# Log-sparse attention block with a spiking feed-forward: ScalarE measures four groups of entering rows and makes all marks, the base product is split in two halves, and every engine's order is rewritten

## The reference

```python
def attn(x):                       # 16 heads of 8
    q, k, v = x @ Wq.T + bq, x @ Wk.T + bk, x @ Wv.T + bv
    scores = where(mask, q . k, 0.0) / sqrt(8)   # mask: key j = i, or i - 2**m, m = 0..9
    return softmax(scores) @ v @ Wo.T + bo       # masked keys keep weight exp(0)
def ffn(x):
    y = square(relu(x @ W_fc.T)) @ W_proj.T      # 128 -> 512 -> 128
    # five leaky steps with threshold 1 and reset; the mean number of spikes
    return count_of_spikes(y) / 5
x = x + layernorm(attn(layernorm(x)))
x = x + layernorm(ffn(layernorm(x)))
```

## Time and profile before

| what | value |
|---|---|
| median of 3 runs | 229.02 us |
| the profiled execution's own time | 228.11 us |
| its span in the trace | 226.3 us |
| mean granted clock of TensorE | 0.91 of full |
| PE busy | 184.1 us (81%) |
| DVE busy | 180.6 us (80%) |
| POOL busy | 161.8 us (72%) |
| ACT busy | 111.6 us (49%) |
| DMA | 30.51 MB, mean 135 GB/s |

### The profile page before, as it was taken

The page is one execution under the profiler, slowest core; times in us unless marked ns, Lnnn a source line. Parts: engine busy times, 40 slices in busy tenths (PEclk is TensorE's granted clock), DMA queues, the critical chain, the costliest instruction groups (busy, mean ns, idle before and its releaser), DMA issues.

```text
span 226.3 us, 3606 instructions
## 1 busy us (share of the span) xinstructions
PE 184.1 (81%) x1108; PEld 93.4 (41%) x1108; DVE 180.6 (80%) x451; ACT 111.6 (49%) x311; POOL 161.8 (72%) x197
## 2 busy tenths in 40 slices
PE   7688985739090998778999999499997799999961
PEld 2223523212020643532645634364464366364840
DVE  5869999999999959999569986760598679866562
ACT  2354755410010035595589468315982725655980
POOL 7342228776799959999999999489297997835031
PEclk9969999985769569999999999758999999999997
DMA  6920000599897899983944399798586710100002
GB/s 183 263 66 0 0 3 1 146 212 216 197 217 197 209 233 225 232 183 107 219 104 127 86 224 234 218 227 209 130 198 142 158 33 0 49 1 23 26 24 69
DMA packets 18388, 30.51 MB, mean 135 GB/s; under 512 B 2753, under 2 KB 15042, under 8 KB 16322
## 3 DMA queue, kind: packets, MB, share of 16 engines
q10 hardware_dynamic: 4176, 22.22, 43.3%
q1 hardware_dynamic: 14194, 8.07, 13.3%
HBM read 25.17 MB, written 5.11 MB: 134 GB/s over the span
## 4 chain that ended last, share of the span: by engine, by line
PE 30%; POOL 28%; DVE 16%; DMA 10%; issue 9%; ACT 3%; ACTq 1%; SPq 1%; POOLq 1%; DVEq 0%
POOL ws L662 15%; DMA packed<-wt 8%; DVE qk L869 5%; PE xbank L1187 5%; PE xbank L1178 5%; PE xbank L1168 4%; POOL wt L601 3%; PE xbank L1163 3%; POOL wt L612 3%; DVE qk L875 3%; DVE ws L930 2%; DMA x_all<-x 2%; PE q_bank L1178 2%; PE q_bank L1187 2%; PE v_bank L1178 2%
## 5 line engine op out<-in xcount | busy, mean ns | idle before, releaser
L662 POOL TENSOR_TENSOR ws<-ws 128x1024 f32<-128x1024 f32 (+1 forms) x36 | 76.2, 2117 | 8.0 <-DVE ws L930 7.4
L930 DVE TENSOR_TENSOR ws<-v_bank,ws 128x896 f32<-128x896 f32 (+4 forms) x54 | 48.0, 905 | 3.8 <-DMA ws<-packed 3.8
L1137 PE MATMUL scores<-qk,head_sum 128*32 128x512 f32 (+1 forms) x256 | 28.0, 573 | 6.6 <-DVE es_raw L897 6.3
L1187 PE MATMUL xbank<-hid,wproj 128*128 128x512 f32 (+1 forms) x56 | 26.8, 577 | 1.2 <-ACT hid L799 1.2
L869 DVE SCALAR_TENSOR_TENSOR qk<-q_bank,bias_cols,kT 128x512 f32<-128x512 f32 (+9 forms) x40 | 24.8, 688 | 2.0 <-ACT kT L722 1.9
L1178 PE MATMUL xbank<-xnT_ff,wfc 128*128 128x512 f32 (+1 forms) x48 | 24.3, 598 | 1.8 <-ACT xnT_ff L713 1.2
L875 DVE SCALAR_TENSOR_TENSOR qk<-q_bank,bias_cols,kT 128x1024 f32<-128x1024 f32 x20 | 24.3, 1266 | 0.3 <-issue 0.2
L1168 PE MATMUL xbank<-wo,ws 128*64 128x128 f32 x264 | 23.9, 319 | 0.0
L1163 PE MATMUL xbank<-wo_base,ws_base 17*128 17x128 f32 x52 | 14.9, 373 | 9.9 <-POOL ws L662 6.7
L799 ACT ACTIVATE hid<-hid 128x512 f32<-128x512 f32 (+1 forms) x36 | 20.7, 581 | 1.6 <-POOL ws L662 1.1
L793 ACT ACTIVATE hid<-xbank 128x512 f32<-128x512 f32 (+1 forms) x24 | 13.4, 559 | 12.6 <-PE xbank L1178 8.0
(11 more groups left out here) (146 smaller groups left out, 345.9 us busy)
## 6 DMA issues: line engine op xcount, KB each, us to landing
ws<-packed ACTq DMA_DIRECT2D x16, 1024.0 KB, 7.6
ws<-packed ACTq DMA_DIRECT2D x4, 768.0 KB, 10.7
packed<-wt SPq DMA_DIRECT2D x16, 128.0 KB
ws<-packed ACTq DMA_DIRECT2D x4, 512.0 KB, 5.8
x_all<-x SPq DMA_DIRECT2D x7, 256.0 KB, 5.3
out<-x_all SPq DMA_DIRECT2D x7, 256.0 KB, 2.3
packed<-wt SPq DMA_DIRECT2D x4, 96.0 KB
x_all<-x SPq DMA_DIRECT2D x2, 128.0 KB, 3.3
```

Of the source, the lines that this page charges most:

```text
L662: e.tensor_tensor(out=a, in0=a, in1=b, op=ALU.add).then_inc(merged, 1)
L930: return v.tensor_tensor(out=w, in0=steps_of(tokens, o - o2, slots, [CH, i1 - i0], [1, CH]), in1=w, op=ALU.mult)
L1137: last = t.matmul(scores[32 * j:32 * j + 32, k, :], head_sum[:, half, :], qk[:, u % 2, k, tok:tok + CH], start=half == 0, stop=half == 1)
L1187: last = t.matmul(bank[:, 0:n], wproj[:, f, :], hid[:, g % 2, f, 0:n], start=f == 0, stop=f == FB - 1)
```

## The change

- `ON_DVE["in"] = (0, 1, 2, 7, 8)`: for entering groups 3, 4, 5, 6 DVE no longer measures the rows. ACT does, in the new stage `powers_in`: four Identity activations that accumulate the row sums, one that turns the sums into negative means, four Square activations with that mean as bias that accumulate the variance. POOL's `rsqrt in` then reads `power`, and for these groups makes no negative mean.
- `ON_DVE["marks"] = ()`: the marks of groups 4, 5, 6 are made by ACT (Sign) and no longer by DVE.
- `ON_POOL["square"] = (8,)`: the four squares of group 8 move from ACT to POOL. `FOLD = (7,)`: in group 7 POOL adds one more slot to another, and the attention there has one slot less.
- The base product of each block is issued as two products of 64 tokens, each 64 columns wide in its stationary operand.
- The warm-up is 28 matmuls of 256 columns on a tile of its own (before: 14 of 512). The `neg_ident` constant and the unused stage `shift` of PE are gone. `KEEP` is empty, so the new stage `keep_up` never runs.
- All five orders are rewritten, with other PSUM banks. Near the start, SP loads `wo` before the second group of `x` and the ffn weights after it; DVE makes both products, max and shift of unit 0 with only the measures of groups 7 and 8 between them, and starts weights 0 in the middle of unit 2's products; POOL's sum of unit 0 stands ahead of its differences, behind five `rsqrt in` where seven stood; ACT has `powers in` 3 and 4 around norm in 2, and 5 and 6 around the first spreads.

```diff
 ON_DVE = {
-    "marks": (4, 5, 6),
+    "in": (0, 1, 2, 7, 8),
+    "marks": (),
...
-ON_POOL = {"square": (), "sum": (0, 1, 2, 3)}
-FOLD = ()
-WARM = 14
+ON_POOL = {"square": (8,), "sum": (0, 1, 2, 3)}
+FOLD = (7,)
+WARM, KEEPS = 28, 8
...
 DVE_ORDER = (
...
+    ("centred bo", 0), ("centred fc", 0), ("moments in", 2), ("products 0", 0), ("products 1", 0),
+    ("moments in", 7), ("max", 0), ("moments in", 8), ("shift", 0), ("products 0", 1),
+    ("inverse", 0), ("products 1", 1), ("max", 1), ("shift", 1), ("products 0", 2), ("inverse", 1),
+    ("weights 0", 0), ("products 1", 2), ("weights 1", 0), ("max", 2), ("weights 2", 0),
...
             def rsqrt_in(g):
                 rsqrt("in", g)
+                if g not in ON_DVE["in"]:
+                    return
...
+            def powers_in(g):
+                u, first, n = IN_GROUPS[g]
+                done = upto(ON_DVE["in"], g, False)
+                act.wait_ge(x_in[g], 16)
...
+                for i in range(n):
+                    last = s.activation(squares["in"][:, i, :], rows(IN_GROUPS[g])[:, i, :], ACT.Identity,
+                                        accum_out=row_sums[:, g, i:i + 1])
...
+                s.activation(neg_mean[:, u, first:first + n], row_sums[:, g, 0:n], ACT.Identity,
+                             scale=-1.0 / (D * float(np.sqrt(D)))).then_inc(mean_by_act, 1)
...
+                for i in range(n):
+                    last = s.activation(squares["in"][:, i, :], rows(IN_GROUPS[g])[:, i, :], ACT.Square,
+                                        scale=1.0 / float(np.sqrt(D)), bias=neg_mean[:, u, first + i:first + i + 1],
+                                        accum_out=power["in"][:, g, i:i + 1])
...
-                    t.matmul(bank[:, cols], ws_base[:, h, (first + i) * P:(first + i + 1) * P],
-                             wo_base[:, u // 2 % 2, :], start=True, stop=False)
+                    for half in range(2):
+                        tok = (first + i) * P + CH * half
+                        t.matmul(bank[CH * half:CH * half + CH, cols], ws_base[:, h, tok:tok + CH],
+                                 wo_base[:, u // 2 % 2, :], start=True, stop=False)
```

The new orders around the end and the middle, as far as the prediction speaks of them:

```diff
 ACT_ORDER = (
...
+    ("square 0", 5), ("square 1", 5), ("signs", 4), ("relu 2", 5), ("norm ff", 6),
+    ("relu 3", 5), ("square 2", 5), ("square 3", 5), ("turned ff", 6), ("signs", 5), ("norm ff", 7),
...
+    ("square 3", 7), ("signs", 6), ("relu 0", 8), ("relu 1", 8), ("relu 2", 8), ("relu 3", 8),
+    ("signs", 7), ("signs", 8),
 POOL_ORDER = (
...
+    ("normalise 2", 5), ("rsqrt mid", 3), ("merge 1", 4), ("normalise 0", 6), ("merge 2", 4),
+    ("normalise 1", 6), ("merge 3", 4), ("normalise 2", 6), ("rsqrt ff", 3), ("rsqrt out", 1),
...
 PE_ORDER = (
...
+    ("up 2", 8, 4), ("down 2", 7), ("up 3", 8, 5), ("count", 6, 3), ("down 3", 7), ("down", 8, 0),
+    ("down 1", 8), ("down 2", 8), ("down 3", 8), ("count", 7, 1), ("count", 8, 4),
```

More of the change, by code:

```diff
@@ L88 @@
[L88 to L91, removed]
+    ("rsqrt in", 0), ("rsqrt in", 1), ("rsqrt in", 2), ("rsqrt in", 3), ("rsqrt in", 4), ("sum", 0),
+    ("differences", 0), ("normalise 0", 0), ("normalise 1", 0), ("normalise 2", 0), ("rsqrt in", 5),
@@ L92 @@
+    ("rsqrt ff", 7), ("rsqrt mid", 8), ("rsqrt out", 5), ("rsqrt ff", 8), ("square 0", 8),
+    ("square 1", 8), ("square 2", 8), ("square 3", 8), ("rsqrt out", 6), ("rsqrt out", 7),
+    ("rsqrt out", 8),
 )
 ACT_ORDER = (
-    ("norm in", 0), ("norm in", 1), ("turned in", 0), ("turned in", 1), ("keys", 0), ("norm in", 2),
-    ("turned in", 2), ("norm in", 3), ("keys", 1), ("turned in", 3), ("norm in", 4), ("norm in", 5),
-    ("total", 0), ("keys", 2), ("turned in", 4), ("base", 0), ("turned in", 5), ("keys", 3),
@@ L97 @@
[L97 to L114, removed]
@@ L115 @@
-    ("powers out", 2), ("signs", 3), ("spread 1", 7), ("norm ff", 4), ("turned ff", 4),
[8 rows of a table removed]
-    ("square 1", 8), ("signs", 7), ("relu 2", 8), ("square 2", 8), ("relu 3", 8), ("square 3", 8),
-    ("signs", 8),
+    ("norm in", 0), ("turned in", 0), ("norm in", 1), ("turned in", 1), ("keys", 0),
+    ("powers in", 3), ("norm in", 2), ("powers in", 4), ("turned in", 2), ("norm in", 3),
+    ("keys", 1), ("norm in", 4), ("exp", 0), ("turned in", 3), ("total", 0), ("turned in", 4),
+    ("keys", 2), ("base", 0), ("powers in", 5), ("total", 2), ("keys", 3), ("spread 0", 0),
@@ new lines @@
+    ("base", 2), ("norm in", 5), ("exp", 1), ("spread 1", 0), ("turned in", 5), ("spread 2", 0),
+    ("powers in", 6), ("keys", 4), ("norm in", 6), ("turned in", 6), ("spread 0", 1), ("exp", 2),
+    ("total", 4), ("spread 1", 1), ("keys", 5), ("spread 2", 1), ("norm in", 7), ("exp", 3),
+    ("spread 0", 2), ("powers mid", 0), ("spread 1", 2), ("spread 2", 2), ("powers ff", 0),
+    ("turned in", 7), ("keys", 6), ("exp", 4), ("spread 0", 3), ("norm ff", 0), ("spread 1", 3),
+    ("powers mid", 1), ("turned ff", 0), ("base", 4), ("norm in", 8), ("relu 0", 0),
@@ new lines @@
+    ("spread 2", 3), ("relu 1", 0), ("square 0", 0), ("relu 2", 0), ("square 1", 0),
+    ("turned in", 8), ("square 2", 0), ("powers ff", 1), ("relu 3", 0), ("keys", 7),
+    ("spread 0", 4), ("exp", 5), ("norm ff", 1), ("square 3", 0), ("spread 1", 4),
+    ("powers mid", 2), ("turned ff", 1), ("signs", 0), ("relu 0", 1), ("spread 2", 4),
+    ("relu 1", 1), ("square 0", 1), ("powers out", 0), ("square 1", 1), ("norm ff", 2),
+    ("relu 2", 1), ("exp", 6), ("square 2", 1), ("relu 3", 1), ("square 3", 1), ("spread 0", 5),
@@ new lines @@
+    ("powers mid", 3), ("spread 1", 5), ("turned ff", 2), ("relu 0", 2), ("square 0", 2),
+    ("signs", 1), ("relu 1", 2), ("square 1", 2), ("powers out", 1), ("spread 0", 6),
+    ("spread 2", 5), ("norm ff", 3), ("relu 2", 2), ("spread 1", 6), ("square 2", 2), ("relu 3", 2),
+    ("turned ff", 3), ("square 3", 2), ("powers mid", 4), ("relu 0", 3), ("exp", 7), ("relu 1", 3),
+    ("square 0", 3), ("relu 2", 3), ("square 1", 3), ("signs", 2), ("total", 6), ("relu 3", 3),
+    ("square 2", 3), ("base", 6), ("square 3", 3), ("spread 2", 6), ("norm ff", 4), ("spread 0", 7),
@@ L133 @@
[L133 to L138, removed]
@@ L157 @@
+    ("residual", 8), ("moments ff", 8), ("final", 5), ("moments out", 6), ("final", 6),
+    ("moments out", 7), ("moments out", 8), ("final", 7), ("final", 8),
 )
 PE_ORDER = (
-    ("warm", 0, 0), ("centre qkv", 0, 2), ("centre fc", 0, 1), ("turn in", 0, 0), ("turn in", 1, 2),
-    ("queries", 0), ("keys", 0, 0), ("values", 0), ("turn in", 2, 1), ("values", 1), ("keys", 1, 2),
-    ("turn in", 3, 0), ("scores 0", 0), ("queries", 1), ("scores 1", 0), ("keys", 2, 1),
-    ("total", 0, 2), ("turn in", 4, 0), ("base", 0), ("turn in", 5, 1), ("keys", 3, 0),
@@ L179 @@
[L179 to L180 removed]
[7 rows of a table removed]
[L188 removed]
+    ("warm", 0, 0), ("centre qkv", 0, 2), ("turn in", 0, 1), ("centre fc", 0, 0), ("turn in", 1, 2),
+    ("keys", 0, 1), ("values", 0), ("queries", 0), ("turn in", 2, 0), ("scores 0", 0),
+    ("scores 1", 0), ("keys", 1, 2), ("values", 1), ("turn in", 3, 1), ("queries", 1),
@@ L1202, in count, with keep_up @@
                 last.then_inc(count_filled, 1)
+            def keep_up(i):
+                what, u, j = KEEP[i]
+                bank = bank_for("keep", i)
+                if what == "products":
+                    pe.wait_ge(qk_ready, 2 * u + j + 1)
+                elif what == "max":
+                    pe.wait_ge(max_ready, u + 1)
+                else:
+                    pe.wait_ge(wv_ready, wv_before(u) + j + 1)
+                for _ in range(KEEPS):
+                    last = t.matmul(bank[:, 0:2 * P], warm_x[:, 0:P], warm_x[:, :], start=True, stop=True)
+                last.then_inc(kept, 1)
             def warm_up(u):
```

191 lines of the change are left out of this document (90 added, 101 removed), and 34 rows, old and new, of tables (ACT_ORDER, PE_ORDER).

## The result

The changed kernel takes 215.71 us (median of four, 212.72 to 218.01) against 228.8 (228.38 to 229.28): the ratio is 0.9368, with a 95% interval of 0.9312 to 0.9425. Two later groups of runs gave the same program 213.21 (`after_again`) and 216.44 us (`after_third`), ratios 0.9288 [0.9231, 0.9346] and 0.9268 [0.919, 0.9346]. A ratio and its interval compare only the fast runs of each kernel, those at most 1.5% above its fastest, while the times in us are medians of all its runs, so that the two need not agree: by the medians the three ratios are 0.943, 0.934 and 0.949.

A forecast was written before the change was run, and what follows sets the result against it. Bound by DVE at the start, POOL and DVE in the middle, PE at the end. Last merge of group 4 at 130.5 + 80.7 + 5.2 - 3.0 - 0.4 = 213.0 span, plus 1.8 outside: 214.8, said as 215 us; range 205 to 226.

The forecast's parts named there:

- Start: DVE's list before the first merge: 16.0 us less work, 3 us given to waits, first merge at 45 instead of 58.15.
- my 22 us more for ACT: ACT's added busy time: 14.4 us for four measures plus 9.0 for the marks, less 1.6.
- the 16 us: DVE work gone between unit 0's first products and its weights 1: measures, products of units 3 and 4, max and shift.
- Middle: POOL from first merge to last merge of group 4: 4.0 us more work, yet that merge ends at 130.5, 9.2 earlier.
- my own sign: Between start and middle: the prediction falls if the first merge is early but attention 4 is not.
- the transfers take the gain: Rival on the DMA queues: late units' packs wait as before, leaving only PE's 3.4 us and perhaps 1; 224 us, chance 0.15.
- End: PE from attention 4 to the span's end: 80.7 us, plus 5.2 moved work, minus 3.0 for the base and 0.4 FOLD.
- The base: PE's base product as two halves: 0.22 us in place of 0.41, saving 0.19 a block, 3.0 for 16 blocks.
- the 5.2 us of work that moved behind attention 4: On PE: an up and two down products of group 2, a turn, unit 7's second scores, total and base.
- ACT as head of the line: Rival: ACT, over nine tenths busy in groups 4 to 8, holds up relus and spreads; 231 to 236 us, chance 0.13.
- Orders as planned: Rival: PE runs from attention 4 to the end at high clock without waits, 9 us better; 206 us, chance 0.14.
- The halves do not overlap: Rival on PE's base: two halves cost one full product, losing 3 us; 218 us, sharing 0.58 with the forecast.

The follow-up runs named there:

- measures_on_dve: The changed kernel with only the measures of groups 3, 4, 5 and 6 back on DVE; 215.16 us, ratio 0.9334 to the kernel before.
- full_base: The changed kernel with only the base product put back in one full-width piece; 213.37 us, ratio 0.9317 to the kernel before.
- later_spreads: The changed kernel with spread 2 of unit 2 and spread 1 of unit 4 later in ACT's list; 213.36 us, ratio 0.9275 to before.

## Why the prediction held, and which of its steps did not

215 was forecast and 215.7 measured, and the mechanism of the start and of the middle is the one forecast. That the number fits so closely is in part luck: terms of the sum were off both ways, and 215.7 is a median over executions with a late pack, which the sum had not counted, and without. Two signs that I had named as speaking against me did come: ACT stood over 5 us at a spread in the middle, and POOL ran idle between 60 and 130.

**Start: right, by two errors that cancel.** First merge forecast at 45, measured 45.7. DVE's waits before it were some 5 us and not 3; the largest, before max 0, is 2.79 us for PE's scores. In return the products of unit 0 began at 12.17 and not at 13.99; what of the loads, the warm-up or PE's order brought this, no run separates. In `after_again` the merge ran at 46.97. The cover of ACT's measures held: DVE waited 0.18 us for the products of unit 1 (25.47). A measure took ACT 3.1 us (15.36 to 18.45) in place of my 3.6; that is 2.0 of the difference between my 22 us more for ACT and the 17.7 measured, and the rest I have not worked out (DVE: 12.7 less, 14 forecast). My cost of DVE's part, 1.2 us each, was an upper bound of what moving it brings: `measures_on_dve` gave back at most 2.8 us at the first merge and 0.7 points at the end. Most of the 16 us are the order's: products of unit 3 and of unit 4 now stand behind weights 0 and 1.

**Middle: right where the packs land in time.** I put the last merge of group 4 at 130.5 and attention 4 at 131 to 135. It started at 131.85 in `after_again`, 130.11 in `full_base`, 130.67 in `later_spreads`, but at 137.47 in the profiled execution of the changed kernel and at 137.02 in that of `after_third`. For these two the step fails by my own sign: the first merge is early and attention 4 is 2 us and more behind its range. What comes between is one stretch of ACT's queue. The changed kernel, ACT's and POOL's timelines:

```profile
67.88 11.02 ACTq L493 DMA_DIRECT2D ws<-packed  x2
79.02 0.40 ACT L796 ACTIVATE squares_ff<-x_all,neg_mean 128x128 bf16<-128x128 f32 x1 [11.21 <-DMA packed<-wt]
...
84.96 1.55 POOL L594 TENSOR_TENSOR wt<-es 128x640 f32<-128x640 f32 x1 [2.88 <-ACT es L745]
```

`after_again`, the same instructions:

```profile
69.79 5.75 ACTq L493 DMA_DIRECT2D ws<-packed  x2
75.67 0.40 ACT L796 ACTIVATE squares_ff<-x_all,neg_mean 128x128 bf16<-128x128 f32 x1 [6.94 <-POOL ws L655]
```

These are the second and third spread of unit 2. In the changed kernel's trace what they wait for last is a pack, in `after_again` it is a merge of POOL's. In one execution the two issues take 5.75 us, in the other 11.02 (and 10.44 in the profiled one of `after_third`, 218.81); behind them stand `powers ff`, turned in 7, the keys of unit 6 and exp 4, so POOL and DVE (4.00 us before the products at 85.11) run dry. A second such pack of 7.38 us at 100.93 costs POOL 3.40. From the first merge to attention 4 it took 91.7 us, in `after_again` 84.9; 4.2 of these 6.9 us are left in the span. That is the rival "the transfers take the gain", which I had given 0.15: its mechanism is real, it strikes in part of the executions, and takes 4 us and not 9. It goes with the spread from 210.5 to 218.8 among the times of one program: of nine traces of the changed kernel and its near variants, the three with such a stay of over 10 us are those of 218.01, 218.81 and 221.92 (`measures_on_dve`), and the six without took 211.11 to 214.88. What makes a pack late at equal lists is open: I have no row that tells it from the spreads that share the engines.

**End: 82.5 forecast, 79.9 measured** (131.85 to 211.7; 78.4 in the changed kernel's first trace). Three terms were off. The base was mis-sized: 0.19 for a block, measured 0.04, 2.4 us too much. Against it, I had kept the half clock at attention 4. PE's timeline of the changed kernel:

```profile
137.47 0.43 PE L1167 MATMUL xbank<-wo_base,ws_base 17*64 17x128 f32 x4 [0.52 <-POOL ws L655]
137.84 0.66 PE L1172 MATMUL xbank<-wo,ws 128*64 128x128 f32 x8
138.42 0.43 PE L1167 MATMUL xbank<-wo_base,ws_base 17*64 17x128 f32 x4
```

A block takes 0.95 us (0.8 forecast), where it had been 1.77: 3.3 us for four blocks. Before, PE had stood 3.13 us for ACT there and ran at 1.2 GHz behind that (granted clock 0.50 from 146 to 150); now it waits 0.52 us and the granted clock is 1.00 from 90 to 210. Fewer waits for ACT, the 0.8 of the squares among them, make up the other 1.7: behind the start of attention 4 PE's rows show 4.84 us of them before and 2.97 in `after_again`; whether the 5.2 us of work that moved behind attention 4 was sized right, no run separates. On the base the inference failed, not the row: one more slot of four half-width instructions does cost 0.22, but such a slot follows others of its own form, with a contraction of 128 rows, and a base of 17 rows at the start of a block did not behave like it. The base and the slots are now of one width, and the time stays. The Trainium skill (TensorEngine Tiling (Array Packing), When to Use Tiling) counts a small contraction as a case for a tiling of its own, by rows; if the base of 17 rows runs in one, it still changes the mode beside slots of 128 rows, and the drain that the same page's Key Properties tell of would stay where it was. I had looked at the columns only. The 0.04 us fit this reading, but no row shows the mode, and no run here has a base of 128 rows, which would test it.

**ACT as head of the line** (0.13): no. ACT is busy 8.36 of 10 us at 200 to 210 with the marks, and 8.68 at 190 to 200; in `after_again` it is 9.39 there, over the nine tenths I had named, and still PE waits only 0.38 us for it in these ten. The longest wait of PE for ACT behind attention 4 is 1.14. So the busy share was no good sign. That marks cost the same on either engine (3.00 us on ACT, 3.08 on DVE) held. That the move is therefore worth nothing held only beside the old list, in which PE waits for no mark of DVE's; in the new one the marks left on DVE cost 2.4 us, by the weights of group 8 behind them. The Trainium skill's rule (ScalarE: Activation LUTs, Rules for kernel authors) names relu, max, min, add and multiply and gives VectorE's lead for bf16; these marks are comparisons of f32 rows, and show no such lead.

**Orders as planned** (206): in part. The 3 us of the clock and 1.9 of the waits came, but the base gave back 2.4; the lowest time of the changed kernel in any group is 210.46. **The halves do not overlap** (218, counted with the forecast): true but for 0.04 a block, and paid for by the clock.

## What to carry to other kernels

Cost a reordering by listing what stands between two fixed points on the limiting engine, before and after, and adding prices of rows: this gave 45 for 45.7 to 47.0 and 130.5 for 131.7, but 137.3 where a pack came late. The orders were worth some seven tenths of the gain or more, and no single move of work between engines more than about 2%. Two stages of equal price on two engines are not equal for what is queued behind them: follow that to the engine that limits. An instruction's price in another form can't be had by subtraction between rows; use the nearest row of its own contraction and place, or give the term a wide bound. A DMA issue in the list of a computing engine ties that engine to what the issue waits for, here a pack or a merge: read its stay in the queue in more than one execution before trusting one trace.

## What the runs showed of the hardware

A matmul of 17 rows of contraction costs 0.41 us for two of full width and 0.37 for four of half width at 2.4 GHz, with the slots of half width behind it in both. Five marks of 128x512 take 3.0 to 3.1 us on ACT and on DVE alike. An accumulating activation of 128x128 f32 on ACT comes every 0.29 us (Identity) or 0.39 us (Square with a bias). The same two DMA issues stood 5.75, 10.44 and 11.02 us in three executions of one program.
